# Attention scores from two f32r parts in two row tiles instead of three bf16 parts

## The reference

```python
xn = layernorm(x)
q = (xn @ Wq).reshape(B, S, 16, 16)       # 16 heads of 16
k = (xn @ Wk).reshape(B, S, 8, 16)        # 8 heads, each for two of q's; v alike
scores = q @ k.T / 4 + where(mask, 0, -10000)   # causal & (last 128 keys | landmark)
s = softmax(scores) @ v @ Wo
g = silu(gelu(xn @ w1_q.T + b1) @ w2_q.T + b2)  # w1, w2 made ternary: -1, 0, 1
out = x + s * g
```

## Time and profile before

| | us |
|---|---|
| median of 3 runs | 742.63 |
| span of the profiled execution | 740.2 |
| PE busy | 632.2 (85%), 4336 matmuls |
| ACT busy | 475.4 (64%) |
| DVE busy | 374.9 (51%) |
| Pool busy | 88.3 (12%) |
| score matmuls (line 735) | 197.3 us, 768 |
| values matmuls (line 755) | 165.6 us, 1536 |
| mask matmuls (line 742) | 103.8 us, 576 |

### The profile page before, as it was taken

The page is one execution under the profiler, slowest core; times in us unless marked ns, Lnnn a source line. Parts: engine busy times, 40 slices in busy tenths (PEclk is TensorE's granted clock), DMA queues, the critical chain, the costliest instruction groups (busy, mean ns, idle before and its releaser), DMA issues. The chain is left out here.

```text
span 740.2 us, 11752 instructions
## 1 busy us (share of the span) xinstructions
PE 632.2 (85%) x4336; PEld 357.2 (48%) x4336; DVE 374.9 (51%) x1000; ACT 475.4 (64%) x723; POOL 88.3 (12%) x94
## 2 busy tenths in 40 slices
PE   1226866999999979999999769999999899799982
PEld 1215752664455456554454636654554556334532
DVE  4976972574827444676545615748364521410101
ACT  1021245678776866687778655697768656888680
POOL 5600020020010021020100201110100210201001
PEclk9656776999999999999999969999999799899996
DMA  7000298200127359001091748001082690020101
GB/s 213 0 0 1 40 115 135 43 8 9 58 36 94 53 79 203 20 7 31 30 107 31 95 130 113 12 8 57 23 108 40 83 157 15 8 89 8 51 10 49
DMA packets 46833, 43.84 MB, mean 59 GB/s; under 512 B 6065, under 2 KB 41394, under 8 KB 46770
## 3 DMA queue, kind: packets, MB, share of 16 engines
q1 hardware_dynamic: 44642, 41.18, 33.4%
q10 hardware_dynamic: 2128, 1.84, 0.8%
HBM read 11.28 MB, written 4.19 MB: 21 GB/s over the span
## 5 line engine op out<-in xcount | busy, mean ns | idle before, releaser
L829 ACT ACTIVATE probs<-sc_ps,shift 128x512 f32<-128x512 f32 (+1 forms) x288 | 175.6, 616 | 98.7 <-PE sc_ps L742 98.0
L735 PE MATMUL sc_ps<-q_stack,k_stack 99*128 99x512 bf16 (+3 forms) x768 | 197.3, 342 | 29.3 <-PEq L209 10.2
L832 ACT ACTIVATE probs<-sc_ps,key_bias 128x1024 f32<-128x1024 f32 (+3 forms) x256 | 204.6, 817 | 16.9 <-PE sc_ps L735 16.3
L755 PE MATMUL att_ps<-probs,v_sb 128*32 128x512 f32 (+3 forms) x1536 | 165.6, 503 | 0.0
L735 PEld LDWEIGHTS sc_ps<-q_stack,k_stack 99*128 99x128 bf16 x768 | 49.9, 99 | 177.2 <-ACT probs L832 65.0
L742 PE MATMUL sc_ps<-near_mask,mask_ident 128*128 128x256 bf16 (+1 forms) x576 | 103.8, 264 | 0.0
L867 POOL TENSOR_TENSOR h_lo<-hid,h_hi 128x512 fp32r<-128x512 f32 x32 | 43.1, 1347 | 338.4 <-DVE h_hi L899 338.4
L742 PEld LDWEIGHTS sc_ps<-near_mask,mask_ident 128*128 128x128 bf16 x576 | 55.7, 101 | 36.8 <-issue 6.7
L682 PE MATMUL aux_ps<-w2T,h_hi 128*128 128x256 f32 x256 | 70.1, 307 | 0.0
L682 PE MATMUL aux_ps<-w2T,h_lo 128*128 128x256 f32 x256 | 63.2, 279 | 0.0
L790 ACT ACTIVATE hid<-aux_ps,b_sb 128x512 f32<-128x512 f32 x64 | 43.0, 687 | 22.5 <-PE aux_ps L672 14.7
(11 more groups left out here) (152 smaller groups left out, 776.8 us busy)
## 6 DMA issues: line engine op xcount, KB each, us to landing
q_stack<-q_parts SPq DMA_DIRECT2D x96, 128.0 KB, 8.2
k_stack<-k_parts SPq DMA_DIRECT2D x24, 256.0 KB, 8.8
xn<-in_L_attn_hidden_states SPq DMA_DIRECT2D x4, 1024.0 KB, 9.2
attT<-att_raw SPq DMA_DIRECT2D x128, 32.0 KB
rden_bc<-den SPq DMA_DIRECT2D x64, 64.0 KB
probs<-in_L_ffn_w SPq DMA_DIRECT2D x2, 1024.0 KB, 7.7
out_y<-xn SPq DMA_DIRECT2D x4, 512.0 KB, 6.5
xn<-in_L_attn_hidden_states SPq DMA_DIRECT2D x3, 512.0 KB, 4.0
```

The costliest lines, as they stand in the source:

```text
L735: last = pe.matmul(sc_ps[:, 2 * u + hh, lo:CH], k_stack[0:KROWS + SHIFT_ROWS, h // REP, kb * P:(kb + 1) * P], q_stack[0:KROWS + SHIFT_ROWS ...
L755: last = pe.matmul(att_ps[32 * q:32 * q + 32, n % 2, lo:CH], v_sb[:, kb, j * VW:j * VW + 32], probs[:, i % 3, q, lo:CH], start=(kb == 0), ...
L829: last = act.activation(probs[:, i % 3, us, lo:near], sc_ps[:, us, lo:near], ACT.Exp, bias=shift[:, 0:1], scale=HD ** -0.5)
L832: last = act.activation(probs[:, i % 3, us, near:CH], sc_ps[:, us, near:CH], ACT.Exp, bias=key_bias[:, kb:kb + 1], scale=HD ** -0.5)
```

## The change

- q and k are split into two f32r parts instead of three bf16 parts. Three products are stacked (hi x hi, hi x lo, lo x hi): 48 rows a head, and two shift rows, 50 in all.
- Two heads of a pair stand at rows 0 and 64 of the stacks (RT), so that their matmuls use the upper and the lower half of the array's rows. The stacks have 8 and 4 slots of f32r instead of 16 and 8 of bf16: the same bytes. The moving operand is f32r of 50 rows instead of bf16 of 99, the stationary one too.
- The columns of the projection weights are reordered for that in 14 pieces instead of 4. The four heads of a group lie in another order in the banks; values reads them so.
- After a projection DVE does one operation instead of three.
- k_parts shares the space of the first half of q_parts. So q is projected at C1 + 5, 7, 9 and 11, and k at C1 + 21 and C1 + 23, with a wait of ACT until q's first half is stacked.
- In the prologue DVE sets all of q_stack to 0 and all of k_stack to 1, ahead of its other work. Pool's two memsets go. The raw weights lie in rden_bc, att_raw and mean_row.
- In the first turn SP stacks q before k.
- row_maxima is changed to match; it doesn't run here.

```diff
-    NPART = 6
-    QPART = [0, 1, 2, 0, 1, 0]
-    KPART = [0, 0, 0, 1, 1, 2]
+    NPART = 3
+    QPART = [0, 0, 1]
+    KPART = [0, 1, 0]
-    SHIFT_ROWS = 3
+    SHIFT_ROWS = 2
+    RT = P // 2
...
-        q_parts = sb("q_parts", [P, QT, 3, S], BF16)
-        k_parts = sb("k_parts", [P, 3, S], BF16)
-        q_stack = sb("q_stack", [P, H, S], BF16)
-        k_stack = sb("k_stack", [P, KVH, S], BF16)
+        q_parts = sb("q_parts", [P, QT, 2, S], F32R)
+        k_parts = q_parts[:, :, :, 0:CH]
+        q_stack = sb("q_stack", [P, SLOTS, S], F32R)
+        k_stack = sb("k_stack", [P, KSLOTS, S], F32R)
...
-                lk(pool.memset(q_stack[KROWS:KROWS + 32, :, :].bitcast(F32), 0.0))
-                lk(pool.memset(k_stack[KROWS:KROWS + 32, :, :], 1.0))
...
+                dve.memset(q_stack[:, :, :].bitcast(F32), 0.0)
+                lk(dve.memset(k_stack[:, :, :].bitcast(F32), 1.0))
...
-                jobs += [(s + 5 + c, "k_proj", c) for c in range(NC)]
                 jobs += [(s + at, "q_proj", m, c) for (m, c), at in zip(((0, 0), (1, 0), (0, 1), (1, 1)),
-                                                                         (6, 8, 10, 12) if main else (7, 8, 9, 10))]
+                                                                         (5, 7, 9, 11) if main else (5, 6, 7, 8))]
+                jobs += [(s + (21 + 2 * c if main else 9 + c), "k_proj", c) for c in range(NC)]
...
                         for i in range(NPART):
-                            for m in range(QT):
-                                sp.dma_start(q_stack[i * HD:(i + 1) * HD, m * HT:(m + 1) * HT, cs],
-                                             q_parts[:, m, QPART[i], cs]).then_inc(stack_in[c], 16)
+                            for f in range(2):
+                                for m in range(QT):
+                                    sp.dma_start(q_stack[f * RT + i * HD:f * RT + (i + 1) * HD, m * QM:(m + 1) * QM, cs].bitcast(F32),
+                                                 q_parts[f * RT:(f + 1) * RT, m, QPART[i], cs].bitcast(F32)).then_inc(stack_in[c], 16)
...
-                        for hh in range(2):
-                            h = g * NQ + 2 * u + hh
-                            last = pe.matmul(sc_ps[:, 2 * u + hh, lo:CH], k_stack[0:KROWS + SHIFT_ROWS, h // REP, kb * P:(kb + 1) * P],
-                                             q_stack[0:KROWS + SHIFT_ROWS, h, c * CH + lo:(c + 1) * CH], start=True, stop=(near == lo))
+                        for f in range(2):
+                            rows = slice(f * RT, f * RT + KROWS + SHIFT_ROWS)
+                            last = pe.matmul(sc_ps[:, 2 * u + f, lo:CH], k_stack[rows, g, kb * P:(kb + 1) * P],
+                                             q_stack[rows, 2 * g + u, c * CH + lo:(c + 1) * CH], start=True, stop=(near == lo))
...
-                            ins = dve.tensor_tensor(resid[:, :], ps, part[0], ALU.subtract)
-                            ins.then_inc(aux_free[bank], 1)
-                            dve.wait_ge(aux_free[bank], before_it + 1)
-                            lk(dve.tensor_copy(part[1], resid[:, :]))
-                            ins = dve.tensor_tensor(part[2], resid[:, :], part[1], ALU.subtract)
...
+                            dve.tensor_tensor(part[1], ps, part[0].bitcast(F32), ALU.subtract).then_inc(q_split, 1)
```

More of the change, by code:

```diff
@@ L236, in layer_norm, with w_columns, slot_of @@
                 lk(dve.tensor_copy(rstd[:, :], root[:, 0:T]))
[L238 to L245, removed]
+        def w_columns():
+            for lo in range(0, NW, P):
+                for k in range(KD):
+                    src, parts = w_nat[:, k, lo:lo + P], [w[:, k, lo:lo + P] for w in (wqkv_hi, wqkv_lo)]
+                    if lo >= D + P:
+                        yield src, parts
+                        continue
+                    for f in range(2):
+                        if lo < D:
+                            own = src.rearrange("p (a f r) -> p f a r", a=2, f=2)[:, f].rearrange("p a (u d) -> p a u d", d=HD)
+                            to = [w.rearrange("p (f r) -> p f r", f=2)[:, f].rearrange("p (d a u) -> p a u d", a=2, u=2) for w in parts]
+                        else:
+                            own = src.rearrange("p (s f d) -> p f s d", f=2, d=HD)[:, f]
+                            to = [w.rearrange("p (f r) -> p f r", f=2)[:, f].rearrange("p (d s) -> p s d", d=HD) for w in parts]
+                        yield own, to
+        def slot_of(h):
+            return (h % NQ) // 2, 2 * (h // NQ) + h % 2
+        W_PIECES = len(list(w_columns()))
         with nc.Block(no_gpsimd_drain=True) as block:
@@ L266, in _ @@
                 act.wait_ge(wqkv_in, 48)
-                for lo in range(0, NW, P):
-                    src, (hi, _) = w_columns(lo)
+                for src, (hi, _) in w_columns():
                     act.activation(hi, src, ACT.Copy).then_inc(w_first, 1)
@@ L326, in _ @@
                     dve.tensor_reduce(wsum[:, n, T:T + 1], wsum[:, n, 0:T], AX_X, ALU.add).then_inc(wabs_done, 1)
-                dve.wait_ge(w_first, NW // P)
-                for lo in range(0, NW, P):
-                    src, (hi, low) = w_columns(lo)
+                dve.wait_ge(w_first, W_PIECES)
+                for src, (hi, low) in w_columns():
                     dve.tensor_tensor(low, src, hi.bitcast(F32), ALU.subtract)
@@ L431, in _ @@
                                   allow_small_or_imprecise_dtypes=True).then_inc(index_done, 1)
+                @block.vector
+                def _(dve):
+                    dve.memset(row_max, 0.0)
                 @block.tensor
@@ L456, in _ @@
                                 pe.wait_ge(masked_done, h - 1)
+                            f, slot = slot_of(h)
+                            rows = slice(f * RT, f * RT + KROWS)
                             for half in range(NC):
-                                last = pe.matmul(sc_ps[:, 2 * (h % 2) + half, :], q_stack[:, h, bass.ds(t * P, P)],
-                                                 k_stack[:, h // REP, half * CH:(half + 1) * CH], start=True, stop=True)
+                                last = pe.matmul(sc_ps[:, 2 * (h % 2) + half, :], q_parts[rows, 0, slot // TC, (slot % TC) * P:(slot % TC + 1) * P],
+                                                 k_stack[rows, h // NQ, half * CH:(half + 1) * CH], start=True, stop=True)
                             last.then_inc(sc_done, 1)
@@ L493, in _ @@
                         for r in range(SHIFT_ROWS):
-                            sp.dma_start(q_stack[KROWS + r:KROWS + r + 1, :, bass.ds(t * P, P)],
-                                         parts[:, r, :]).then_inc(max_in, 16)
-                        sp.wait_ge(max_in, 16 * SHIFT_ROWS)
+                            for h in range(0, H, 2):
+                                f, slot = slot_of(h)
+                                row = f * RT + KROWS + r
+                                sp.dma_start(q_stack[row:row + 1, slot:slot + 2, bass.ds(t * P, P)].bitcast(F32),
+                                             parts[h:h + 2, r, :].bitcast(F32)).then_inc(max_in, 16)
+                        sp.wait_ge(max_in, 16 * SHIFT_ROWS * H // 2)
                 clear_semaphores()
@@ L755, in values @@
                             last = pe.matmul(att_ps[32 * q:32 * q + 32, n % 2, lo:CH], v_sb[:, kb, j * VW:j * VW + 32],
[L756 removed]
+                                             probs[:, i % 3, 2 * (q % 2) + q // 2, lo:CH], start=(kb == 0), stop=(kb == TC * (c + 1) - 1))
                         last.then_inc(pv_done, 1)
```

71 lines of the change are left out of this document (38 added, 33 removed).

## The result

The changed kernel takes 788.09 us (median of 4 runs, 782.53 to 791.51) against 742.25 for the kernel before on the same chip: a ratio of 1.061, 95% interval 1.056 to 1.065. A second set of runs gave 788.72 (783.55 to 793.26), 1.059 (1.052 to 1.065). The direction is the forecast one, the size is not: 751 had been expected, and 788 lies outside 699 to 766. The profiled span is 786.4 us, 46.2 above the 740.2 of before, where the sum said 8.2.

What follows compares the result with a forecast made beforehand. PE's stream was taken to bound the main turns, and DVE waiting for Pool the path ahead of 117 us. Terms +24 - 12.8 + 2 - 3 - 2 = +8.2 on 742.6 gave 751 us, range 699 to 766.

Steps and rivals of the forecast that it cites:

- Saved streams, switches, weight loads: Main turns: -14.2 us streams, +12.1 mode switches, +9.2 and +0.7 loads a full turn; +29.7 over four turns.
- rival 2: Score pairs: the row tiles don't overlap, so a pair costs two f32r streams, +16 us a turn; 815 us, chance 0.08.
- rival 1: Main turns: no drain between whole array and row tiles, so the kernel is faster; 701 us, chance 0.24.
- I give 1.5 us a turn back: Main turns: some added time falls where PE waits anyway, at turns' first steps and unmasked last-turn steps; +29.7 becomes +24.
- The preparing turn, -5: Preparing turn: about -3 us from projections with fewer DVE operations, and -2 from a denser PE that may keep the clock.
- its copy waits for the DMAs of q that were issued some ten steps before: k's projection, 16 steps later: its copy waits for q's DMAs, issued some ten steps before; no cost was added.
- The prologue, -10.8: Prologue: Pool's memsets go, -12.8 us on the path; DVE's clearing of whole stacks costs 0 to 8, taken as +2.
- Rival 3: Prologue: DVE's clearing holds Pool and the broadcast comes 8 us late; 757 us, inside the range, no chance given.
- the prediction called 13 the point from which it is wrong: Prologue: DVE's memsets ending past 13 us was listed among the signs that the prediction is wrong.

Runs made afterwards that it cites:

- same_tile: Kernel after, but both heads of a pair use the row tile at row 0 (half the scores wrong): 879.74 us, ratio 1.184.
- mask_tiles: Kernel after, but the mask matmuls also run as halves in the two row tiles (mask wrong): 764.17 us, ratio 1.027.
- b_mask_tiles: Kernel before, with only its mask matmuls run in two row tiles (mask wrong): 790.06 us, ratio 1.063.
- whole: Kernel after, but each score matmul contracts rows 0 to 113 on the whole array, without row tiles (scores wrong): 780.09 us, ratio 1.049.
- whole_own: Kernel after, with whole-array scores (wrong) and a place of its own for k in the preparing turn: 763.51 us, ratio 1.027.
- own_k0: Kernel after, but in the preparing turn k's parts lie in a buffer of their own, not over q's first half: 772.24 us, ratio 1.040.
- b_dve_pads: Kernel before, but DVE clears the pads ahead of its other work instead of Pool: 739.72 us, ratio 0.995.

## Why the prediction was right or wrong

The sum was to be +8.2 us of span and was +46.2: 38.0 short, in three places.

**Saved streams, switches, weight loads: right in kind and in sum.** The second tile costs next to nothing, by same_tile (0.22 us more for a pair in one tile, a stream of the earlier trace rows being 0.233); that was rival 2, and it is out. The switch between whole array and row tiles costs the 0.095 us of the switch to column tiles: mask_tiles takes that away between scores and masks, and b_mask_tiles adds it alone, at +46 us. That was rival 1, and it is out. The exposed weight load is the remainder of 0.31 at 256 columns: 0.31 - 0.117 - 0.095 = 0.10. The working gave 29.7 us over 48 steps in four turns, 26.0 for 42 of 48; measured 26.6, in which are the 2.4 us behind ACT's wait and some 3 us of clock in the last turn, so that this part is if anything a few us below the working.
The Trainium skill, TensorEngine Tiling (Array Packing), section Key Properties, says that changing the tiling mode, and not just the tile, drains the engine. Measured, it agrees for row tiles as well as for column tiles, at 0.095 us. The Trainium skill, TensorE: Matmul & The Clock Gate, Part 3, has a factor of 3.07 for four row tiles; these runs have two only, and for them the streams are halved (0.22 us less for a pair of 512 columns than in one tile), which agrees with tiles that run at the same time. No run here has four.

What decided here is that a stream of 0.06 to 0.23 us stands between two switches.

**"I give 1.5 us a turn back": wrong, and with the wrong sign.** Outside steps 5 to 47 the working left 29.7 - 26.0 - 6 = -2.3 us, and 16.4 came: 18.7 of the 38.0. The step that failed is the term for the turns' starts: it took 6 us off for waits that would hide the longer stream, and put the half clock there at nothing, as if of unchanged length. Over whole turns the half clock went from 53 to 90 us. Of the 37 us more, some 26 lie in the first five steps, where PE is busy throughout (17.48 of 17.62 us in the last turn), so that half of them, 13 us, is time; those steps grew by 13.5. What is left of the 16.4, 3.4 us, is near the 3.7 that the working had there before it took the 6 off: nothing shows them saved.

That the two long spells belong to the kernel is shown by its second profile. That they go with the row tiles is shown in part: whole, which has neither the row tiles nor their switches, doesn't have them and is 8.0 us faster, and whole_own is 8.7 us below own_k0 by the medians, but 2.4 by the profiled executions. Whether a turn's start has its long spell varies (own_k0 has it in the first turn and not in the last two), masks in the tiles shorten the sum to 70, and the kernel before itself moves between 53 and 66 with when its turns start. So the experiments tie some 8 us to the tiles, and what lengthens the spells stays open.

**The preparing turn, -5: wrong by 16.3.** From the first row of the layer norm to the first scores it took 79.5 us before and takes 90.8. The step that failed is "its copy waits for the DMAs of q that were issued some ten steps before". It was said of the main turn alone; the same wait in the preparing turn, where k follows q's last projection by one job, was not looked at, though the change makes ACT wait there too. own_k0 shows its whole cost, 18.4 us at the first scores, of which 13.5 are the wait and the rest goes with the clock that PE has behind it. The sentence isn't right for the main turn either: SP issues these DMAs from 223.85 us, in step 34, three steps before k's projection and not ten, so ACT does stand for them, 3.8 to 4.2 us a turn. PE has a job to do meanwhile, so little of that reaches it: 2.4 us in three turns. With the wait gone, in own_k0, the preparing turn is 2.1 us better than had been worked out.

**The prologue, -10.8: 2.7 too good.** Rival 3 was not it: Pool's broadcast came at 15.86 as against 15.74. DVE's long operations went with Pool's memsets, as the prediction read them. The clearing itself was priced too low, by the rate of a TENSOR_SCALAR (2048 in 1.29 us) and from the start of the span. DVE starts at 2.58, the memsets take 10.35 together with 0.8 between, and end at 13.74; the prediction called 13 the point from which it is wrong. The thresholds are 4.7 us late (21.67 against 16.97) instead of 2: that is the 2.7. Behind them 12.8 us are saved, as worked out.

The three come to 37.7 of the 38.0 us. The direction is no luck: 26.6 us more in the steps against 8.1 less in the prologue would have made the kernel slower without the two large misses. The range was too narrow on its upper side because both large misses were costs put down as at or under nothing, with no bound above them. Above 766 stood only the 0.08 of rival 2, and nothing for a wait that the change adds.

## What to carry to other kernels

Before matmuls are packed into tiles of the array, count the changes of mode on PE in program order: at 0.095 us a change and 0.10 for each f32r weight load behind it, a pair must save more than 0.2 us of streaming, which two heads of 512 columns only just reach (0.44 us from a pair to its masks before and after). A change of type moves the loads as well: without any row tiles the f32r version still cost 28 us in the steps. When one buffer takes over the space of another, walk the new wait through every place where the code runs, the short preparing pass first, where the distance is one job, and count in the main pass from where the DMAs are issued. An engine that is idle anyway (here ACT, while weights load) is the one to clear buffers: that alone was worth 1.6%, and is the fastest version measured.

## What the runs showed of the hardware

- A change between whole array, 64-row tiles and 32-column tiles costs some 0.1 us (0.09 to 0.11), at 128 as at 256 columns: scores to masks 0.22 for 0.11 us at 128 (b_mask_tiles against the earlier trace rows), 0.31 for 0.22 at 256 (the kernel after against mask_tiles), masks to values 0.21 for 0.11 at 128.
- The first f32r weight load behind such a change costs another 0.10 us: 0.22 from scores of 256 columns to their masks in mask_tiles, without a switch between them, where the stream is 0.117.
- PE can work without a gap and stay at half clock: for 16 us at the start of two turns in the kernel after, for 40 us in same_tile (760 to 800, clock 0.50). Over the main turns the granted clock was at the half level for 52 to 66 us in the six profiled executions whose scores use the whole array, and for 70 to 161 in the five that use row tiles. What decides it is open.
- A memset of DVE over 8192 elements has a row of 6.88 us on 32 partitions of bf16 and on 128 of f32 alike, and the next one started 7.7 us (the kernel after) and 8.5 us (b_dve_pads) after it; Pool's row is 6.92, and ACT's copy of one broadcast element takes 7.02. Beside Pool's memset DVE's TENSOR_SCALAR from SBUF to SBUF took 6.29 us and ended with it; beside ACT's copy the same one took 0.17.
